# Routed experts of a two-layer gated block: gate and up weights as the stationary operand, token weights applied at the output

## What is computed

```python
h = silu(x @ gate_w.T) * (x @ up_w.T)      # 256 -> 176
acc = acc + w[:, None] * (h @ down_w.T)    # 176 -> 256, w: the token's weight for this expert
```

## Time and profile before

| | |
|---|---|
| time, median of 3 runs | 927.02 us (926.72 to 927.92) |
| span of the profiled execution, first to last instruction | 924.4 us |
| outside the span, by the median | 2.6 us |
| expert stage of layer 0 | 198.2 to 287.5 us |
| expert stage of layer 1 | 673.4 to 835.9 us |
| tail behind it | 835.9 to 924.4 us |

### The profile page before, as it was taken

How to read it: one execution, slowest core, us unless ns; L and a number is a source line. 1 busy time by engine, 2 the same in 40 slices (tenths; PEclk the granted TensorE clock), 3 DMA queues, 4 the chain that set the end, 5 groups by cost and what they waited for, 6 DMA issues and landing times.

```text
span 924.4 us, 18404 instructions
## 1 busy us (share of the span) xinstructions
PE 725.4 (78%) x5700; PEld 487.8 (53%) x5701; DVE 682.8 (74%) x1825; ACT 440.6 (48%) x1037; POOL 505.8 (55%) x607
## 2 busy tenths in 40 slices
PE   3469747678999798577788777668699999999990
PEld 1258635356675355244444444344567777775650
DVE  4968957756775776999988999648867777773574
ACT  3365415323332123699888999634033344342330
POOL 5284894547663838555553557010164444468885
PEclk9678975979999899779877887758989999999995
DMA  8034444724443211599999999820034444455445
GB/s 297 1 88 152 145 143 155 231 75 132 146 147 104 82 56 46 112 182 177 192 175 196 200 185 179 151 91 8 10 113 139 131 131 137 139 151 120 80 92 154
DMA packets 205754, 121.17 MB, mean 131 GB/s; under 512 B 146476, under 2 KB 197808, under 8 KB 205680
## 3 DMA queue, kind: packets, MB, share of 16 engines
q1 hardware_dynamic: 192816, 91.10, 40.8%
q0 software_dynamic: 12864, 29.14, 12.7%
HBM read 64.16 MB, written 32.98 MB: 105 GB/s over the span
## 4 chain that ended last, share of the span: by engine, by line
PE 27%; POOL 9%; DVE 9%; ACT 9%; issue 7%; DMA 4%; DVEq 2%; POOLq 1%; ACTq 0%; SPq 0%
PE PS L269 13%; ACT sb_xnf L1417 4%; PE PS L852 4%; POOL sb_region L713 4%; DVE sb_wk L1450 3%; DMA sb_xnf<-sb_xnf 3%; ACT sb_wkh L1417 3%; PE PS L791 2%; POOL sb_stg L713 2%; PE PS L815 2%; PE PS L844 2%; PE PS L1344 2%; POOL sb_xnf L713 1%; PE PS L407 1%; POOL sb_wqp L713 1%
## 5 line engine op out<-in xcount | busy, mean ns | idle before, releaser
L673 POOL DMA_INDIRECT sb_xnf<-token_table,sb_ids x120 | 115.9, 966 | 149.1 <-DVE sb_wk L1018 63.1
L1450 DVE TENSOR_SCALAR_CACHE_REDUCE sb_wk<-PS 128x512 f16<-128x512 f32 x256 | 161.7, 684 | 8.2 <-PE PS L1344 7.6
L269 PE MATMUL PS<-sb_xnT,sb_sgu 128*128 128x512 f16 x528 | 126.2, 391 | 1.1 <-DVE sb_lg L455 0.6
L269 PE MATMUL PS<-sb_region,sb_wkh 128*128 x720 | 120.2, 318 | 5.6 <-issue 3.2
L875 ACT ACTIVATE sb_wk<-PS 128x512 f32<-128x512 f32 (+1 forms) x48 | 28.6, 596 | 140.8 <-PE PS L269 128.1
L269 PEld LDWEIGHTS PS<-sb_region,sb_wkh 128*128 128x128 f16 x720 | 68.8, 99 | 46.7 <-issue 14.6
L1417 ACT ACTIVATE sb_xnf<-PS,sb_slotv 128x512 int16<-128x512 f32 x128 | 87.0, 704 | 11.9 <-DVE sb_wk L1450 7.9
L1417 ACT ACTIVATE sb_wkh<-PS,sb_slotv 128x512 int16<-128x512 f32 x128 | 87.4, 707 | 10.8 <-DVE sb_wk L1450 8.7
L269 PEld LDWEIGHTS PS<-sb_xnT,sb_sgu 128*128 128x128 f16 x528 | 52.4, 100 | 58.7 <-issue 7.5
L791 PE MATMUL PS<-sb_sdn,sb_wkh 128*128 128x256 f16 x544 | 69.4, 279 | 16.9 <-DVE sb_wkh L989 15.1
L1018 DVE SCALAR_TENSOR_TENSOR sb_wk<-PS,sb_sm,sb_wk 128x176 f32<-128x176 f32 x120 | 42.6, 397 | 52.7 <-ACT sb_wk L903 52.6
(11 more groups left out here) (296 smaller groups left out, 1682.3 us busy)
## 6 DMA issues: line engine op xcount, KB each, us to landing
slot_table<-sb_wa SPq DMA_DIRECT2D x60, 256.0 KB
slot_table<-token_table SPq DMA_DIRECT2D x16, 640.0 KB
sb_stg<-gu SPq DMA_DIRECT2D x24, 352.0 KB, 4.1
sb_stg<-dn SPq DMA_DIRECT2D x24, 256.0 KB, 3.6
token_table<-sb_xnf SPq DMA_DIRECT2D x16, 256.0 KB, 4.8
sb_stg<-sgu SPq DMA_DIRECT2D x8, 352.0 KB, 5.3
sb_x_sb<-x SPq DMA_DIRECT2D x1, 2048.0 KB, 12.2
out<-sb_x_sb SPq DMA_DIRECT2D x16, 128.0 KB, 2.5
```

The lines of the kernel that those rows point to most:

```text
L269: last = nc.tensor.matmul(out_, lhs(i, c), rhs(j, c), start=(c == 0 and n == 0 and not begun), stop=(c == C - 1 and n == 2 and not more))
L673: nc.gpsimd.indirect_dma_start(xg[l][:, 2 * (g % XR) + n, :], None, xw[l][:, :], bass.IndirectOffsetOnAxis(ap=ids[:, 2 * g + n:2 * g + n + ...
L1450: nc.vector.tensor_scalar(h_any[(2 * s + h) % 6], PS[:, (2 * s + h) % LB, :], LEVELS, None, ALU.add, ALU.min, accum_out=h_nb[s % 3][:, h:h ...
```

## The change

- Gate and up: the weights become the stationary operand and the transposed tokens the moving one. The 352 columns of an expert (176 gate, 176 up) are reordered on the host into 112 gate, 112 up, 64 gate, 64 up, and are taken in three windows of 128 columns (`WINDOWS`); two neighbouring windows share 16 columns. That makes 18 matmuls of 128 columns for each tile, in place of 6 of 352.
- The inner layer comes out with its 176 values in the partitions. PE's four transposes of it and their semaphore `e_hT` go, and the high and low halves are made from SBUF by one copy on ACT and two subtractions on DVE.
- The tokens' weights no longer multiply the inner layer. ACT applies them as a scale per partition when it copies the finished rows out of PSUM, in two instructions; that copy leaves DVE. Its step moves from `s-2` to `s-3`, and the down product gets two PSUM banks.
- One tiny scaling in routing and one clearing of a buffer go.

```diff
-    EREM = EI - P
+    EREM = P // 2
+    EFULL = EI - EREM
...
-        LOW_AT = P // 2
-        DOWN_PARTS = ((P, 0, 0, 0), (P, 0, 0, 1), (P, 1, 0, 0), (LOW_AT + EREM, 0, 1, 0), (LOW_AT + EREM, 0, 1, 1))
+        DOWN_PARTS = ((EFULL, 0, 0, 0), (EFULL, 0, 0, 1), (EFULL, 1, 0, 0), (P, 0, 1, 0), (P, 0, 1, 1))
+        WINDOWS = ((0, 0, 0), (EFULL, 0, 2 * P), (EG - P, 1, 0))
...
                     at_least(pe, e_xl[l], base, s + 1)
+                    at_least(pe, e_h[l], base, s - 1)
                     for n in range(2):
-                        last = mm3(PS[:, 2 * u + n, 0:EG], lambda i, c: wkh[:, 2 * u + i, (2 * n + c) * P:(2 * n + c + 1) * P],
-                                   lambda h, c: GU[l][:, bass.ds(e[n], 1), h, c, :].rearrange("p o n -> p (o n)"))
+                        for first, bank, at in WINDOWS:
+                            last = mm3(PS[:, 2 * u + bank, at + n * P:at + (n + 1) * P],
+                                       lambda h, c: GU[l][:, bass.ds(e[n], 1), h, c, first:first + P].rearrange("p o n -> p (o n)"),
+                                       lambda i, c: wkh[:, 2 * u + i, (2 * n + c) * P:(2 * n + c + 1) * P])
                     last.then_inc(e_gu[l].sem, 1)
-                at_least(pe, e_hl[l], base, s - 1)
-                if inside(base, s, 1, NG[l] + 1):
-                    at_least(pe, e_h[l], base, s)
-                    for n in range(2):
-                        for c in range(C):
-                            last = nc.tensor.transpose(PS[:, 6, (2 * c + n) * P:(2 * c + n + 1) * P],
-                                                       wk1[:, 3 - u, n * EI + c * P:n * EI + (c + 1) * P], idf[:, :])
-                    last.then_inc(e_hT[l].sem, 1)
                 if inside(base, s, 2, NG[l] + 2):
                     e = experts(base, s - 2)
-                    at_least(pe, e_y[l], base, s - 2)
+                    at_least(pe, e_hl[l], base, s - 1)
+                    at_least(pe, e_y[l], base, s - 3)
...
             def group(base, s):
                 u = s % 2
+                if inside(base, s, 1, NG[l] + 1):
+                    at_least(act, e_h[l], base, s)
+                    at_least(act, e_d[l], base, s - 2)
+                    nc.scalar.activation(wkh[0:EFULL, 6 - 2 * u, :], wk1[0:EFULL, 3 - u, :], ACT.Copy).then_inc(e_hh[l].sem, 1)
                 if inside(base, s, 0, NG[l] - 1):
                     high_x(base, s + 1)
+                if inside(base, s, 3, NG[l] + 3):
+                    at_least(act, e_d[l], base, s - 2)
+                    at_least(act, e_st[l][1 - u], base * 8, 16 * ((s - 3) // 2))
+                    for n in range(2):
+                        last = nc.scalar.activation(yb[1 - u][:, n * D:(n + 1) * D], PS[:, 7 - u, n * D:(n + 1) * D], ACT.Copy,
+                                                    scale=wv[(s - 3) % XR][:, n:n + 1])
+                    last.then_inc(e_y[l].sem, 1)
...
-                    nc.scalar.activation(wk1[:, u, 0:EG].rearrange("p (n i) -> p n i", n=2), PS[:, 2 * u:2 * u + 2, 0:EI],
-                                         ACT.Silu, scale=1 / SW).then_inc(e_silu[l].sem, 1)
...
+                    nc.scalar.activation(wk1[0:EFULL, u, 0:2 * P], PS[0:EFULL, 2 * u, 0:2 * P], ACT.Silu, scale=1 / SW)
+                    nc.scalar.activation(wk1[0:EREM, u, 2 * P:4 * P], PS[0:EREM, 2 * u + 1, 0:2 * P], ACT.Silu,
+                                         scale=1 / SW).then_inc(e_silu[l].sem, 1)
```

More of the change, by code:

```diff
@@ L325, in gated_flamingo @@
         e_h = both("e_h", NG[0])
-        e_hT = both("e_hT", NG[0])
         e_hh = both("e_hh", NG[0])
@@ L357, in gated_flamingo @@
         table_zeroed = sem("table_zeroed")
-        wv = [sm[:, 12 + u, 0:2] for u in range(2)]
+        wv = [sm[:, 12 + u, 0:2] for u in range(XR)]
         wtmp = [bst2[:, u, :, :] for u in range(2)]
@@ L834, in group @@
                     at_least(pe, e_xl[l], base, s + 1)
+                    at_least(pe, e_h[l], base, s - 1)
                     for n in range(2):
[L836 to L837 removed]
+                        for first, bank, at in WINDOWS:
+                            last = mm3(PS[:, 2 * u + bank, at + n * P:at + (n + 1) * P],
+                                       lambda h, c: GU[l][:, bass.ds(e[n], 1), h, c, first:first + P].rearrange("p o n -> p (o n)"),
+                                       lambda i, c: wkh[:, 2 * u + i, (2 * n + c) * P:(2 * n + c + 1) * P])
                     last.then_inc(e_gu[l].sem, 1)
[L839 to L846 removed]
                 if inside(base, s, 2, NG[l] + 2):
                     e = experts(base, s - 2)
[L849 removed]
+                    at_least(pe, e_hl[l], base, s - 1)
+                    at_least(pe, e_y[l], base, s - 3)
                     for n in range(2):
                         for p, (r, i, c, h) in enumerate(DOWN_PARTS):
[L852 removed]
+                            last = nc.tensor.matmul(PS[:, 6 + u, n * D:(n + 1) * D],
                                                     wkh[0:r, 4 + 2 * u + i, (2 * c + n) * P:(2 * c + n + 1) * P],
@@ L902, in group @@
                     at_least(act, e_h[l], base, s - 1)
-                    nc.scalar.activation(wk1[:, u, 0:EG].rearrange("p (n i) -> p n i", n=2), PS[:, 2 * u:2 * u + 2, 0:EI],
-                                         ACT.Silu, scale=1 / SW).then_inc(e_silu[l].sem, 1)
[L905 to L909, removed]
+                    nc.scalar.activation(wk1[0:EFULL, u, 0:2 * P], PS[0:EFULL, 2 * u, 0:2 * P], ACT.Silu, scale=1 / SW)
+                    nc.scalar.activation(wk1[0:EREM, u, 2 * P:4 * P], PS[0:EREM, 2 * u + 1, 0:2 * P], ACT.Silu,
+                                         scale=1 / SW).then_inc(e_silu[l].sem, 1)
             at_least(act, s_d[l], 0, HALF)
             high_x(0, 0)
-            steps(act, NG[l] + 1, 2, 4, 2, group)
+            steps(act, NG[l] + 3, XR, XR + 1, 4, group)
             at_least(act, e_d[l], 0, NG[l])
@@ L1003, in low_x, with token_weights @@
                                         ALU.subtract).then_inc(e_xl[l].sem, 1)
+            def token_weights(base, s):
+                at_least(dve, e_y[l], base, s - 3)
                 j = slice(2 * (base + s), 2 * (base + s) + 2) if isinstance(base, int) else bass.ds(base * 2 + 2 * s, 2)
@@ L1007, in low_x @@
                 dve.drain()
-                nc.vector.tensor_reduce(wv[v], wtmp[v][:, :, 0:n_], AX, ALU.add)
-                dve.drain()
+                nc.vector.tensor_reduce(wv[s % XR], wtmp[v][:, :, 0:n_], AX, ALU.add)
             def group(base, s):
                 u = s % 2
+                if inside(base, s, 1, NG[l] + 1):
+                    at_least(dve, e_hh[l], base, s)
+                    nc.vector.tensor_tensor(wkh[0:EFULL, 7 - 2 * u, 0:2 * P], wk1[0:EFULL, 3 - u, 0:2 * P],
+                                            wkh[0:EFULL, 6 - 2 * u, 0:2 * P], ALU.subtract)
+                    nc.vector.tensor_tensor(wkh[EREM:2 * EREM, 6 - 2 * u, 2 * P:4 * P], wk1[0:EREM, 3 - u, 2 * P:4 * P],
+                                            wkh[0:EREM, 6 - 2 * u, 2 * P:4 * P], ALU.subtract).then_inc(e_hl[l].sem, 1)
                 if inside(base, s, 0, NG[l] - 1):
@@ L1015, in group @@
                 if inside(base, s, 0, NG[l]):
+                    token_weights(base, s)
+                    dve.drain()
                     at_least(dve, e_silu[l], base, s + 1)
[L1017 to L1033, removed]
+                    nc.vector.scalar_tensor_tensor(wk1[0:EFULL, 2 + u, 0:2 * P], PS[0:EFULL, 2 * u, 2 * P:4 * P], HW / SW,
+                                                   wk1[0:EFULL, u, 0:2 * P], ALU.mult, ALU.mult)
+                    nc.vector.scalar_tensor_tensor(wk1[0:EREM, 2 + u, 2 * P:4 * P], PS[EREM:2 * EREM, 2 * u + 1, 0:2 * P], HW / SW,
+                                                   wk1[0:EREM, u, 2 * P:4 * P], ALU.mult, ALU.mult).then_inc(e_h[l].sem, 1)
             low_x(0, 0)
-            steps(dve, NG[l] + 2, XR, XR, 3, group)
+            steps(dve, NG[l] + 1, XR, XR, 2, group)
             for s in range(HALF, NSH + 3):
@@ L2207, in down_parts, with gate_up_parts @@
     def down_parts(w):
-        rest = w[:, 128:]
-        gap = np.zeros((w.shape[0], 64 - rest.shape[1], w.shape[2]), w.dtype)
-        return np.concatenate([w[:, 0:128], rest, gap, rest, gap], 1)
+        first, rest = w[:, :-64], w[:, -64:]
+        gap = np.zeros((w.shape[0], 128 - first.shape[1], w.shape[2]), w.dtype)
+        return np.concatenate([first, gap, rest, rest], 1)
+    def gate_up_parts(g, u):
+        return np.concatenate([g[..., :-64], u[..., :-64], g[..., -64:], u[..., -64:]], 2)
     n = {}
```

5 lines of the change are left out of this document (2 added, 3 removed).

## The result

The changed kernel takes 1025.88 us (median of 4 runs, 1024.51 to 1027.15), the kernel before 927.05 (926.72 to 927.92): a ratio of 1.1055, 95% interval 1.1031 to 1.1078. It is slower by 10.5%. The forecast was 1022, with a range of 990 to 1055. The profiled execution has a span of 1024.2 us, 99.8 more than before.

A forecast was written before the change was run, and what follows sets the result against it. PE's array (3.8 us a step) and sequencer (3.76) were taken as level; 16 addresses at 0.125 us make 5.76. With 924.4 + 28.3 (layer 0) + 66.8 (layer 1) = 1019.5 us span, plus 2.6, the forecast was 1022 us, range 990 to 1055.

The forecast's parts named there:

- Level today: Expert stage of the kernel before: PE's array needs 3.8 us a step and its sequencer's own work 3.76 us.
- The array after the change: Expert stage: 36 matmuls 0.053 us apart take 1.91 us, transposes save 0.44; array work falls to about 3.5 us a step.
- The address price: Gate and up on PE's sequencer: 0.125 us per address, bounds 0.114 to 0.143; 16 more addresses add 2.0 us a step.
- Loads bare: PE's sequencer: it no longer gets ahead, so nothing covers the register load before the down product, 0.55 us in the median.
- The sum: Whole kernel: steps of 5.76 us make layer 0 28.3 us and layer 1 66.8 us longer; 1019.5 us span, 1022 us forecast.
- ACT and DVE: Expert stage: ACT will have 2.7 us a step and DVE about 3; both fit in 5.76 us and cost nothing.
- Addresses that don't bind: Rival, gate and up on PE's sequencer: addresses cost little over 46 ns, the array sets the step; 910 us, chance 0.05.
- An array that loses far more: Rival on PE's array: the array loses far more than forecast; its size is not in the text; chance 0.09.
- Weight loads that set the pace: Rival, gate and up: 36 loads of 98 ns take 3.5 us; 30 us more, 1052 us, chance 0.05.

The follow-up runs named there:

- the run in the old orientation: The kernel before, tokens still stationary, with the 352 moving columns of gate and up taken as matmuls of 128, 128 and 96 columns: 1021.68 us, ratio 1.1017.

## Why the prediction was right

**Level today.** "The array needs 3.8 us a step, the sequencer 3.76." The loop of eight groups lays the array's part bare at 3.76, and loads saved in the old form buy nothing: there the array is the larger of the two by a little. The sequencer's figure is borne out from the other side: the changed step of 5.85 less 16 x 0.130 leaves 3.77. That it comes so close is partly luck, as it was read from a single step, off lines printed to 0.1 us. What nobody had foreseen is how much the loop takes: six turns fewer (11 to 5) saved 6.6 us, twice 6 x 0.5; the last section has a likely reason.

**The array after the change.** Forecast 1.91 us for gate and up, about 3.5 a step. With the addresses away the starts are (2.17 - 0.22)/35 = 0.056 us apart and the step is 3.54.

**The address price.** Forecast 0.125 us, bounds 0.114 to 0.143; measured 0.130 (3.0/23), and at least 0.12 by half of the addresses taken away. That the price carries over from the moving side to a weight load was the step least covered by rows of the kernel before; the changed kernel's own lines show that it does, and the run in the old orientation has the same price on the moving side.

**Loads bare.** Forecast: "nothing covers the load before the down product". Shown by the idle time of 0.6 to 0.7 us before it, which goes when the load goes.

**The sum.** Four steps and a turn were to take 4 x 5.76 + 0.5 = 23.5 us; they take 791.42 - 767.61 = 23.8. Hence the small misses: layer 0 +29.5 for +28.3, layer 1 +68.5 for +66.8, and the last gather at 916.7 for 911, whose miss also holds the 2.7 us of the start and of the part between the stages that no term covered. The additions kept their pace and still set the end.

**ACT and DVE.** Forecast 2.7 and at most 3.0 us a step; measured 2.5 and 2.7. Off the path, apart from the few us that the output on ScalarE may cost.

**The rivals.** Addresses that don't bind (910) fell: the sequencer shows them at 0.130 each. An array that loses far more (chance 0.09) fell: the granted clock was 0.99 in layer 1's stage, and without addresses the matmuls started 0.056 us apart. Weight loads that set the pace (1052) fell with the same row. That the orientation by itself costs the time fell with the run in the old orientation. The loads as such did not get dearer: 0.54 us, as in the earlier trace rows.

## What to carry to other kernels

Sum the work of PE's sequencer beside the array's. In these kernels each operand window that depends on a register is one address there, some 0.13 us whether 352 or 128 columns follow, and cutting one wide window into three triples them, from 8 a group to 24. The two sums were level here, so the 16 added addresses went onto the path in full (5.85 us a step, against 3.76 where the longer loop hides the turns: 2.09, and 16 x 0.130 = 2.08), while the array's gain went nowhere. Before a load or a loop turn is removed, find out which of the two sums is the larger: the same 46 loads were worth nothing in one kernel and 25 us in the other.

## What the runs showed that was not expected

A register load is not priced by the instruction: two numbers took 0.54 us, six took 0.83 and 1.48 in alternate steps. Why they alternate was not tried.

A loop of eight groups in place of four saved 6.6 us in the kernel before, where the turns seen in its trace (0.5 us each) explained 3. The record shows one thing more that the longer loop takes from the sequencer: 26 of the addresses that the register loads need for themselves. The kernel before, then the same with the longer loop:

```profile
L822 PEldq FUSED_REGOPS  x66: 46/46/60, 214.6 to 811.6; - x66
...
L822 PEldq FUSED_REGOPS  x40: 46/46/60, 688.7 to 805.4; - x40
```

At 0.13 us each these make 3.4, an estimate; with the turns it is 6.4, against 6.6 in the kernel before and 7 in the changed one, where the count falls from 66 to 40 too. No run takes the two apart. In layer 1, from 724 us on, all steps with the longer loop are 3.76 or 3.77 us, so the array hides one turn in eight groups; with a loop of four more than half of the steps there are between 3.96 and 4.27.

With gate and up free of addresses the step was 3.54 us in layer 1, yet the kernel gained only 0.75%. Its trace shows where the rest stayed. Layer 1 up to the last gather became shorter, 809.67 - 675.58 = 134.1 us for 142.6 in the kernel before. Layer 0's stage did not, 288.88 - 198.17 = 90.7 for 89.3: between 199 and 290 us PE waits 12.9 us for gathered rows there, and 1.5 in the kernel before. POOL's additions behind the last gather keep their pace of about 99 us.
